# Ten one-hot products with the operands exchanged: three bfloat16 parts of the weights stationary, x moving 512 columns, sums transposed on TensorE

## The chip, the cores and the metric

One core of a Trainium2 chip runs the whole kernel. The metric is device time in microseconds (us); lower is better. Engines are named as in the profile: PE is TensorE's matmul, PEld its weight load, DVE is VectorE, ACT ScalarE, POOL GpSimd, SP SyncE, whose queue issues the large transfers.

## What is computed

Ten tables with 64 columns each, for a batch of 1024. The reference, cut to what matters:

```python
VOCABS = [12500, 6250, 2500, 1250, 625, 250, 1000, 500, 200, 100]
embs = [jnp.dot(x, w) for x, w in zip(xs, ws)]          # x: 1024 x v, w: v x 64, float32
emb_sum = embs[0]
q_emb = jnp.dot(xs[0] ** 2, ws[0] ** 2)
for i in range(1, len(xs)):
    emb_sum = emb_sum + embs[i]
    q_emb = q_emb + jnp.dot(xs[i] ** 2, ws[i] ** 2)
fm_ans = 0.5 * (emb_sum ** 2 - q_emb)
return jnp.concatenate([fm_ans] + embs, axis=-1)
```

Every x holds only zeros and ones.

## The kernel before, in words

The host hands x over transposed, so that the vocabulary lies on the partitions, 128 rows to a tile. There are 199 tiles, with the last tile of each table cut to a multiple of 16 rows. A tile of x is 128 x 1024 float32 (512 KB); one DMA brings a chunk of one or two tiles into one of SLOTS = 10 slots of `x_ring`. There are 108 chunks, and up to four of them make a group, whose weights come with one DMA from ACT's queue.

Because x is 0 or 1, the upper bfloat16 half of each float32 is x itself, and PE reads it in place (`upper_half`, a stride of two). A weight isn't exact in bfloat16, so each group's `pieces` are made of three summands. ACT squares the weights (`square`, L269), and POOL takes twice the rest that the upper half leaves (L326, L329). The tile `pieces` is laid out kind by kind, weights and squares apart: `[P, 3, 2, GROUP, D]`.

x is the stationary operand. For each tile and each of eight blocks of 128 batch rows PE loads x as 128 x 128 and moves the six parts of the tile through it, 384 columns (L363). The sums of a batch block lie in one PSUM bank, batch on the partitions. Tables are gathered in rounds (`ROUNDS`). The first round holds five small tables, and there and in the last round a tile is multiplied by 24 matmuls of 128 columns (L368), since the three kinds are added up in PSUM. At a round's end ACT copies bank after bank (`copy_out`, L290, L293), while PE's first matmul on each bank in the next round waits for its copy. DVE (`combine`) and POOL (`add_squares`) then add the parts up.

To prove that x holds nothing but 0 and 1, DVE counts ones in each chunk (L433) and ACT counts nonzeros (L276); a general path, which doesn't run with these inputs, stands behind a flag. A slot is filled again when PE, DVE and ACT have all read its chunk (the three waits in `load_x`).

The order on each engine is the order of the code; semaphores alone tie the engines together. The lines behind the two edits that matter most:

```python
            def load_w(group):
                if group.g >= BUFFERS:
                    act.wait_ge(x_multiplied, GROUPS[group.g - BUFFERS].end)
...
                    if c == 0 and group.g + LEAD + 1 < NGROUPS:
                        load_w(GROUPS[group.g + LEAD + 1])
                    if c == min(2, len(group.chunks) - 1) and group.g + LEAD < NGROUPS:
                        square(GROUPS[group.g + LEAD])
```

Of the kernel before, what the change touches and what calls it, by code (L numbers as in the profile page):

```python
# [17 lines left out]
PARTS = 6  # L18
PD = PARTS * D
# [9 lines left out]
ROUNDS = [  # L29
    [(8, [[1, 1]]), (6, [[2, 2, 2, 1, 1]]), (4, [[2, 2, 1]]), (9, [[1]]), (5, [[1, 1]])],  # L30
    [(3, [[2, 2, 2], [2, 1, 1]])],
    [(2, [FULL, [2, 2, 2], [2, 2, 1, 1]])],
    [(1, [FULL] * 6 + [[1]])],
    [(0, [FULL] * 12 + [[1, 1]])],
    [(7, [[2, 1, 1]])],
]
LAST_ROUND = len(ROUNDS) - 1
ORDER = [t for one in ROUNDS for t, _ in one]
LAST = ORDER[-1]
FIRSTS = len(ROUNDS[0])  # L40

Q_PLACE = FIRSTS + 1
PLACE = {t: n + 1 + (n >= FIRSTS) for n, t in enumerate(ORDER)}
CHUNK = max(FULL)
GROUP = sum(FULL)
SLOTS = 10

BUFFERS = 5
LEAD = 2
# [13 lines left out]
class Group:  # L63


    def __init__(self, g, round_, table, tile, sizes, k):
        self.g, self.round, self.table, self.tile = g, round_, table, tile
        self.tiles, self.buffer, self.turn = sum(sizes), g % BUFFERS, g // BUFFERS
        self.chunks, at = [], 0
        for n in sizes:  # L70
            self.chunks.append(Chunk(k + len(self.chunks), table, tile + at, n, at))
            at += n
        for chunk in self.chunks:
            chunk.group = self
        self.end = k + len(sizes)


def plan():
    groups, k = [], 0
    for n, one in enumerate(ROUNDS):  # L80
        for table, lists in one:
            tile = 0
            for sizes in lists:
                groups.append(Group(len(groups), n, table, tile, sizes, k))
                k, tile = groups[-1].end, tile + sum(sizes)
            assert tile == TILES[table] and lists[-1][-1] == 1
    return groups
# [5 lines left out]

BEGINS = [min(c.k for g in GROUPS if g.round == n for c in g.chunks) for n in range(len(ROUNDS))] + [NCHUNKS]
FLAG_MAX = P * NCHUNKS * CHUNK * BATCH


def rec_kernel(nc, xs, ws, out):
# [5 lines left out]
    with ExitStack() as ctx:  # L104
# [12 lines left out]
        pieces = [sb(f"pieces{i}", [P, 3, 2, GROUP, D], F32) for i in range(BUFFERS)]  # L117
        is_one = [sb(f"is_one{i}", [P, CHUNK * BATCH], U8) for i in range(2)]
        is_set = [sb(f"is_set{i}", [P, CHUNK * BATCH], U8) for i in range(2)]
# [6 lines left out]
        ones = sb("ones", [P, 1], F32)  # L126
        stages = [sb(f"stage{i}", [P, NB, PD], F32) for i in range(2)]
        low_sum = sb("low_sum", [P, NB, D], F32)
        q_low = sb("q_low", [P, NB, D], F32)
        q_round = sb("q_round", [P, NB, D], F32)  # L130
        emb_sum = sb("emb_sum", [P, NB, D], F32)
        results = sb("results", [P, NT + 2, NB, D], F32)
        q_total = results[:, Q_PLACE, :, :]
        g_weights = sb("g_weights", [P, 2, D], F32)

        w_landed = [sem(f"w_landed{i}") for i in range(BUFFERS)]
# [6 lines left out]
        pieces_ready = sem("pieces_ready")  # L143
        constants = sem("constants")
        bank_summed = sem("bank_summed")
        bank_copied = sem("bank_copied")
        combined = sem("combined")
        q_combined = sem("q_combined")
        added = sem("added")
        q_added = sem("q_added")  # L150
        half_read = sem("half_read")
        fm_ready = sem("fm_ready")
        last_emb = sem("last_emb")
# [17 lines left out]
        lower, upper = slice(0, NB // 2), slice(NB // 2, NB)  # L171

# [7 lines left out]
        def upper_half(chunk):  # L180

            return in_slot(chunk.slot, chunk.n * BATCH).bitcast(BF16).rearrange(
                "p (t b h) -> p t b h", h=2, b=BATCH)[0:chunk.rows, :, :, 1]

        def piece(group, kind):
            return pieces[group.buffer][:, kind, :, 0:group.tiles, :]

        def piece_upper(group, kind):

            return pieces[group.buffer][:, kind].bitcast(BF16).rearrange(  # L190
                "p m t (d h) -> p m t d h", h=2)[:, :, 0:group.tiles, :, 1]

        def tile_parts(chunk, t):


            return pieces[chunk.group.buffer][0:chunk.rows, :, :, chunk.at + t].bitcast(BF16).rearrange(
                "p k m (d h) -> p k m d h", h=2)[:, :, :, :, 1]

        def wait_bank(eng, n, b):

            if b < NB - 1:
                eng.wait_ge(bank_summed, (NB - 1) * n + b + 1)
            else:
                eng.wait_ge(x_multiplied, BEGINS[n + 1])
# [3 lines left out]
        def _(sp):  # L208
            def load_x(chunk):
# [11 lines left out]
            for chunk in CHUNKS:  # L221
                load_x(chunk)

            for n, one in enumerate(ROUNDS[:-1]):
                sp.wait_ge(added, n + 1)
                for t, _ in one:
                    sp.dma_start(out[t + 1], results[:, PLACE[t], :, :]).then_inc(stored, 16)
# [5 lines left out]
            with sp.If(odd != 0):  # L233
# [15 lines left out]
                sp.dma_start(out[0], results[:, 0, :, :]).then_inc(stored, 16)  # L249
                for t in range(NT):  # L250
# [5 lines left out]
        def _(act):  # L256
# [38 lines left out]

            for group in GROUPS[:LEAD + 1]:
                load_w(group)
# [258 lines left out]
```

## Time and profile before

| | |
|---|---|
| Median of 3 runs | 298.21 us (297.61 to 298.63) |
| Profiled execution, its own time | 298.65 us |
| Its span, first to last instruction | 296.9 us |
| PE busy | 274.8 us (93%) |
| DVE, ACT, POOL busy | 252.5, 230.2, 114.3 us |
| DMA | 113.31 MB, mean 382 GB/s |

Busy time of PE counts matmuls that overlap in the pipeline as busy once. The span leaves out what lies around the instructions, here 1.75 us.

### The profile page before, as it was taken

The numbers are of one execution on the slowest core, as the hardware profiler recorded it, in microseconds if no ns is written. First come the engines' busy times: TensorE is split into PE (matmuls) and PEld (weight loads), VectorE is DVE, ScalarE is ACT, GpSimd is POOL, SyncE is SP. The second block draws the span as 40 slices with busy tenths as digits, with TensorE's granted clock in tenths as the row PEclk, the third lists the DMA queues.
The fourth block names the chain that finished last, engine by engine and source line by source line (L and its number), as shares of the span: only waits on it lengthen the run. The fifth ranks groups of instructions, "written<-read, shape, count | busy, mean of one in ns | idle before, by whom it ended". The sixth has DMA issues, their size and how long they took to land.

```text
span 296.9 us, 5042 instructions
## 1 busy us (share of the span) xinstructions
PE 274.8 (93%) x1946; PEld 169.1 (57%) x1946; DVE 252.5 (85%) x240; ACT 230.2 (78%) x291; POOL 114.3 (39%) x78
## 2 busy tenths in 40 slices
PE   0899779999999999999999999999999999999960
PEld 0899735555555555555555555555555555555660
DVE  3669776899999999997887899998988888987883
ACT  2868499899699878776897878877787788876741
POOL 0911427276518551313618532540451353112060
PEclk9999979999999999999999999999999999999995
DMA  7999999999999999999999999999999999999921
GB/s 241 409 378 367 413 361 383 418 415 309 411 416 417 418 423 414 418 425 300 400 420 414 422 416 417 420 420 418 418 418 421 418 419 419 414 417 280 389 94 75
DMA packets 21435, 113.31 MB, mean 382 GB/s; under 512 B 2656, under 2 KB 3808, under 8 KB 9760
## 3 DMA queue, kind: packets, MB, share of 16 engines
q1 hardware_dynamic: 16800, 106.18, 90.2%
q10 hardware_dynamic: 4608, 6.79, 6.5%
q8 instruction: 16, 0.26, 0.4%
q14 instruction: 11, 0.09, 0.1%
HBM read 110.07 MB, written 2.88 MB: 380 GB/s over the span
## 4 chain that ended last, share of the span: by engine, by line
PE 82%; DMA 10%; DVE 2%; ACT 2%; issue 1%; POOL 0%; ACTq 0%
PE sums L363 81%; DMA x_ring<-in_x_dram 6%; DMA pieces<-in_w_dram 4%; ACT stage L293 1%; PE sums L368 1%; DVE results L450 1%; DVE odd_counts L467 0%; ACT L269 0%; ACT is_set L276 0%; DVE emb_sum L477 0%; DVE low_sum L447 0%; DVE results L483 0%; DVE results L487 0%; DVE results L479 0%; POOL pieces L329 0%
## 5 line engine op out<-in xcount | busy, mean ns | idle before, releaser
L433 DVE TENSOR_SCALAR_CACHE_REDUCE is_one<-x_ring 128x2048 uint8<-128x2048 f32 (+3 forms) x108 | 225.5, 2114 | 37.2 <-DMA x_ring<-in_x_dram 36.9
L363 PE MATMUL sums<-pieces,x_ring 128*128 128x384 bf16 x1416 | 242.1, 332 | 3.8 <-ACT results L290 3.8
L276 ACT ACTIVATE is_set<-x_ring 128x2048 uint8<-128x2048 uint32 (+3 forms) x108 | 192.1, 1787 | 43.9 <-DMA x_ring<-in_x_dram 43.0
L363 PEld LDWEIGHTS sums<-pieces,x_ring 128*128 128x128 bf16 x1416 | 136.5, 97 | 109.1 <-POOL pieces L329 3.9
L326 POOL TENSOR_TENSOR pieces<-pieces 128x1024 f32<-128x1024 f32 (+5 forms) x31 | 48.5, 1566 | 160.1 <-ACT pieces L269 160.1
L329 POOL TENSOR_TENSOR pieces<-pieces 128x1024 f32<-128x1024 f32 (+5 forms) x31 | 49.2, 1588 | 2.4
L368 PE MATMUL sums<-pieces,x_ring 128*128 128x128 bf16 (+2 forms) x528 | 32.7, 225 | 8.4 <-POOL pieces L329 8.4
L368 PEld LDWEIGHTS sums<-pieces,x_ring 128*128 128x128 bf16 (+2 forms) x528 | 32.5, 100 | 8.6 <-issue 8.4
L276 ACT ACTIVATION_READ_ACCUMULATOR is_set<-x_ring 128x1 f32 (+2 forms) x108 | 21.7, 201 | 0.0
L269 ACT ACTIVATE pieces<-pieces 128x512 f32<-128x512 f32 (+5 forms) x31 | 16.8, 545 | 4.7 <-DMA pieces<-in_w_dram 4.7
L293 ACT ACTIVATE stage<-sums 128x384 f32<-128x384 f32 x32 | 12.7, 521 | 2.3 <-PE sums L363 2.3
L335 POOL TENSOR_TENSOR q_low<-stage 128x512 f32<-128x512 f32 x4 | 5.7, 1412 | 10.9 <-ACT stage L293 10.9
L433 DVE DVE_READ_ACCUMULATOR is_one<-x_ring 128x1 f32 (+2 forms) x108 | 8.8, 81 | 0.0
L450 DVE TENSOR_TENSOR results<-low_sum,stage 128x512 f32<-128x512 f32 x4 | 6.9, 1720 | 0.1
L453 DVE TENSOR_TENSOR emb_sum<-emb_sum,results 128x512 f32<-128x512 f32 x4 | 6.9, 1719 | 0.1
L338 POOL TENSOR_TENSOR q_round<-q_low,stage 128x512 f32<-128x512 f32 x4 | 5.5, 1370 | 0.3
L341 POOL TENSOR_TENSOR results<-results,q_round 128x512 f32<-128x512 f32 x4 | 5.5, 1363 | 0.3
L269 ACT ACT_TABLE_LOAD x1 | 1.3, 1283 | 5.4 <-DMA pieces<-in_w_dram 5.4
L447 DVE TENSOR_TENSOR low_sum<-stage 128x512 f32<-128x512 f32 x4 | 4.0, 990 | 1.0 <-ACT stage L293 1.0
L441 DVE TENSOR_REDUCE emb_sum<-results 128x512 f32<-128x2560 f32 x1 | 4.8, 4784 | 0.0
L313 ACT ACTIVATE results<-sums 128x256 f32<-128x256 f32 x2 | 0.8, 384 | 4.6 <-DVE results L479 4.6
L392 PE MATMUL sums<-ones,odd_total 128*1 128x1 f32 x2 | 0.2, 164 | 4.0 <-ACT results L313 4.0
(16 smaller groups left out, 8.8 us busy)
## 6 DMA issues: line engine op xcount, KB each, us to landing
x_ring<-in_x_dram SPq DMA_DIRECT2D x91, 1024.0 KB, 20.0
x_ring<-in_x_dram SPq DMA_DIRECT2D x10, 512.0 KB, 16.4
pieces<-in_w_dram ACTq DMA_DIRECT2D x20, 256.0 KB, 7.3
out_dram<-results SPq DMA_DIRECT2D x10, 256.0 KB, 13.1
x_ring<-in_x_dram SPq DMA_DIRECT2D x4, 448.0 KB, 16.6
x_ring<-in_x_dram SPq DMA_DIRECT2D x2, 320.0 KB, 11.5
pieces<-in_w_dram ACTq DMA_DIRECT2D x3, 192.0 KB, 7.9
x_ring<-in_x_dram SPq DMA_DIRECT2D x1, 384.0 KB, 18.8
```

The costliest lines, as they stand in the source:

```text
L269: nc.scalar.activation(whole[:, 1], whole[:, 0], ACT.Square).then_inc(squared, 1)
L276: nc.scalar.activation(is_set[chunk.k % 2][0:chunk.rows, 0:chunk.n * BATCH], x_of(chunk).bitcast(U32), ACT.Sign, accum_out=set_counts[0:ch ...
L293: nc.scalar.activation(stages[n % 2][:, b, :], sums[:, b, 0:PD], ACT.Copy).then_inc(bank_copied, 1)
L326: nc.gpsimd.tensor_tensor(piece(group, 1), piece(group, 0), piece_upper(group, 0), ALU.subtract).then_inc(rest_ready, 1)
L329: nc.gpsimd.tensor_tensor(piece(group, 2), piece(group, 1), piece_upper(group, 1), ALU.subtract).then_inc(pieces_ready, 1)
L335: nc.gpsimd.tensor_tensor(q_low[:, :, :], stage[:, :, 3 * D:4 * D], stage[:, :, 5 * D:], ALU.add).then_inc(q_combined, 1)
L338: nc.gpsimd.tensor_tensor(q_round[:, :, :], q_low[:, :, :], stage[:, :, D:2 * D], ALU.add).then_inc(q_combined, 1)
L363: return nc.tensor.matmul(sums[:, b, 0:PD], x, parts, start=first, stop=False, skip_group_check=True)
L368: last = nc.tensor.matmul(columns[:, at:q_at + 1:q_at - at, :], x, parts[:, kind], start=first and kind == 2, stop=False, skip_group_check ...
L433: nc.vector.tensor_scalar(is_one[chunk.k % 2][0:chunk.rows, 0:chunk.n * BATCH], x_of(chunk), 1.0, None, ALU.is_equal, ALU.add, accum_out=o ...
L450: nc.vector.tensor_tensor(emb, low_sum[:, :, :], stage[:, :, 0:D], ALU.add).then_inc(combined, 1)
L453: nc.vector.tensor_tensor(emb_sum[:, :, :], emb_sum[:, :, :], emb, ALU.add).then_inc(added, 1)
```

## The change

The operands change places. A tile's weights and squares are now side by side (`[P, 3, GROUP, 2 * D]`), 128 columns to a kind, and each kind is the stationary operand of two matmuls, through which 512 columns of x move. All three kinds are added up in PSUM, in a pair of banks, with the embedding's 64 columns and the squares' 64 on the partitions and the batch along the bank. Each table has its own pair, in turn one of two. After each table ACT copies the pair to SBUF (`copy_sums`), PE transposes it in eight blocks of 128 x 128 float32 (`turn`) into one of two other pairs, ACT copies the embedding out of it (`copy_emb`) and DVE adds embedding and squares to a running total (`add`). These steps are put off by COPY_AFTER, TURN_AFTER and ADD_AFTER chunks from the table's end.

The three weight parts need a buffer that has both halves, so the weights land in `loaded` (3 buffers) and ACT makes two passes, a copy and a square, into `pieces` (4 buffers). SLOTS goes from 10 to 12, the rounds go, and the order of the tables is another.

```diff
-ROUNDS = [
-    [(8, [[1, 1]]), (6, [[2, 2, 2, 1, 1]]), (4, [[2, 2, 1]]), (9, [[1]]), (5, [[1, 1]])],
-    [(3, [[2, 2, 2], [2, 1, 1]])],
...
-    [(7, [[2, 1, 1]])],
-]
-SLOTS = 10
-BUFFERS = 5
-LEAD = 2
+ORDER = [
+    (8, [[1, 1]]),
+    (9, [[1]]),
+    (5, [[1, 1]]),
+    (4, [[2, 2, 1]]),
+    (7, [[2, 1, 1]]),
+    (3, [[2, 2, 2], [2, 1, 1]]),
...
+    (0, [FULL] * 12 + [[1, 1]]),
+    (6, [[2, 2, 2, 1, 1]]),
+]
+SLOTS = 12
+WHOLES = 3
+PAIRS = 4
+AHEAD = 3
+COPY_AFTER, TURN_AFTER, ADD_AFTER = 2, 3, 5
+def due(k, after):
+    return [n for n in range(NT - 1) if min(END[n] - 1 + after, NCHUNKS - 1) == k]
...
+            def square(group):
+                act.wait_ge(w_landed[group.whole], 16 * (group.turn + 1))
+                if group.g >= PAIRS:
+                    act.wait_ge(x_multiplied, GROUPS[group.g - PAIRS].end)
+                w = loaded[group.whole][:, 0:group.tiles, :]
+                nc.scalar.activation(piece(group, 0)[:, :, 0:D], w, ACT.Copy).then_inc(squared, 1)
+                nc.scalar.activation(piece(group, 0)[:, :, D:], w, ACT.Square).then_inc(squared, 1)
+            def copy_sums(n):
+                act.wait_ge(x_multiplied, END[n])
+                if n >= 2:
+                    act.wait_ge(sums_turned, n - 1)
+                at = summing(n, 0)
+                nc.scalar.activation(turned[n % 2][:, :].rearrange("p (a b) -> p a b", a=2),
+                                     sums[:, at:at + 2, :], ACT.Copy).then_inc(sums_copied, 1)
...
+                    if c == min(1, len(group.chunks) - 1):
+                        if group.g + AHEAD < NGROUPS:
+                            load_w(GROUPS[group.g + AHEAD])
+                    if c == min(2, len(group.chunks) - 1) and group.g + AHEAD - 1 < NGROUPS:
+                        square(GROUPS[group.g + AHEAD - 1])
+                    for n in due(chunk.k, COPY_AFTER):
+                        copy_sums(n)
+                    for n in due(chunk.k, ADD_AFTER):
+                        copy_emb(n, ORDER[n][0])
...
+            def multiply(chunk):
+                group, n = chunk.group, chunk.group.place
+                pe.wait_ge(x_landed[chunk.slot], 16 * (chunk.turn + 1))
+                if chunk.k == BEGIN[n] and n >= 2:
+                    pe.wait_ge(sums_copied, n - 1)
+                x = x_upper(chunk)
+                for t in range(chunk.n):
+                    for kind in (2, 1, 0):
+                        w = piece_upper(group, kind)[0:chunk.rows, chunk.at + t, :]
+                        first = chunk.k == BEGIN[n] and t == 0 and kind == 2
+                        for half in range(2):
+                            at = t * BATCH + half * HALF
+                            last = nc.tensor.matmul(sums[:, summing(n, half), :], w,
+                                                    x[:, at:at + HALF], start=first, stop=False,
+                                                    skip_group_check=True)
+                last.then_inc(x_multiplied, 1)
+            def turn(n, blocks):
+                for b in range(blocks.start, blocks.stop):
+                    last = nc.tensor.transpose(turning(n)[:, b, :, :],
+                                               turned[n % 2][:, b * P:(b + 1) * P], identity[:, :])
+                last.then_inc(sums_turned, 1)
```

What this does to the order is seen at two places. The first is PE's start. Before, it multiplied three chunks with nothing but x and `pieces` to wait for:

```order
L368 MATMUL sums<-pieces,x_ring 128x2x64 [waits x_landed0,pieces_ready,constants]
L368 MATMUL sums<-pieces,x_ring 128x2x64 x23
L368 MATMUL sums<-pieces,x_ring 128x2x64 [waits x_landed1]
L368 MATMUL sums<-pieces,x_ring 128x2x64 x23
L368 MATMUL sums<-pieces,x_ring 128x2x64 [waits x_landed2,pieces_ready]
L368 MATMUL sums<-pieces,x_ring 128x2x64 x47
```

Of the changed kernel, PE from its first matmul (`turned` is the SBUF copy of the sums, `identity` a unit matrix):

```order
L361 MATMUL sums<-x_ring,pieces 128x512 [waits parts_ready,x_landed0,unit_ready,constants]
L361 MATMUL sums<-x_ring,pieces 128x512 x5
L361 MATMUL sums<-x_ring,pieces 128x512 [waits x_landed1]
L361 MATMUL sums<-x_ring,pieces 128x512 x5
L361 MATMUL sums<-x_ring,pieces 128x512 [waits x_landed2,parts_ready]
L361 MATMUL sums<-x_ring,pieces 128x512 x5
L361 MATMUL sums<-x_ring,pieces 128x512 [waits sums_copied,x_landed3,parts_ready]
L361 MATMUL sums<-x_ring,pieces 128x512 x5
L361 MATMUL sums<-x_ring,pieces 128x512 [waits x_landed4]
L361 MATMUL sums<-x_ring,pieces 128x512 x5
L368 MATMUL sums<-identity,turned 128x128 [waits sums_copied]
L368 MATMUL sums<-identity,turned 128x128 x7
```

A tile is now 6 matmuls of 512 columns, and the fourth chunk (the third table's first) waits for `sums_copied`, the copy of the first table's sums.

The second place is ACT's queue at the same time. Before, between the counts of the second and the fourth chunk:

```order
L276 ACTIVATE is_set,set_counts<-x_ring 80x1024 [waits x_landed1]
L269 ACTIVATE pieces<-pieces 128x320 [waits w_landed2]
L276 ACTIVATE is_set,set_counts<-x_ring 128x2048 [waits set_counted,x_landed2]
L262 DMA pieces<-in_w_dram 128x128
L276 ACTIVATE is_set,set_counts<-x_ring 128x2048 [waits set_counted,x_landed3]
```

And in the changed kernel, from the second chunk's count to the first `copy_sums` (L287):

```order
L276 ACTIVATE is_set,set_counts<-x_ring 80x1024 [waits x_landed1]
L258 DMA loaded<-in_w_dram 128x320 [waits squared]
L268 ACTIVATE pieces<-loaded 128x2x64 [waits w_landed2]
L269 ACTIVATE pieces<-loaded 128x2x64
L276 ACTIVATE is_set,set_counts<-x_ring 112x1024 [waits set_counted,x_landed2]
L258 DMA loaded<-in_w_dram 128x256 [waits squared]
L268 ACTIVATE pieces<-loaded 128x5x64 [waits w_landed0]
L269 ACTIVATE pieces<-loaded 128x5x64
L276 ACTIVATE is_set,set_counts<-x_ring 128x1024 [waits set_counted,x_landed3]
L287 ACTIVATE turned<-sums 128x1024 [waits x_multiplied]
```

The weights that the copy of 128x5x64 waits for are issued one chunk earlier on the same queue (the row with 128x320), and the copy of the first table's sums stands behind that wait.

## Rows read from the trace of the kernel before

**Rows 1.** The page: span and PE's busy time
```profile
span 296.9 us, 5042 instructions
PE 274.8 (93%) x1946; PEld 169.1 (57%) x1946; DVE 252.5 (85%) x240; ACT 230.2 (78%) x291; POOL 114.3 (39%) x78
PE 82%; DMA 10%; DVE 2%; ACT 2%; issue 1%; POOL 0%; ACTq 0%
```

**Rows 2.** Windows, core 0: start:end, length, busy (instructions) by engine, clock, DMA, GB/s
```profile
8.40:13.00 4.60, 4.55 (x44) 4.58 (x45) 2.90 (x3) 3.76 (x8) 4.52 (x3) 1.00 1.03 416
39.20:43.40 4.20, 4.13 (x16) 1.79 (x17) 3.22 (x3) 4.20 (x8) 0.00 (x0) 0.64 1.07 352
43.40:280.00 236.60, 236.60 (x1395) 134.15 (x1394) 212.64 (x189) 195.01 (x232) 94.69 (x57) 1.00 1.02 404
```

**Rows 3.** Timeline of PE and PEld: start, us, engine, what
```profile
150.25 129.83 PEld L363 LDWEIGHTS sums<-pieces,x_ring 128*128 128x128 bf16 x765 [0.27 <-ACT stage L293]
281.17 5.67 PE L368 MATMUL sums<-pieces,x_ring 128*128 128x128 bf16 x96
281.29 5.55 PE L368 MATMUL sums<-pieces,x_ring 128*128 128x128 bf16 x94
```

**Rows 4.** Waits: us in total, times, longest
```profile
PE sums L368 <- POOL pieces L329: 8.4, 1, 8.4
PE sums L363 <- ACT results L290: 3.8, 1, 3.8
SPq L216 <- PE sums L363: 163.0, 80, 4.9
```

**Rows 5.** Timeline of DVE's counts, late in the run, with idle time before
```profile
252.19 2.29 DVE L433 TENSOR_SCALAR_CACHE_REDUCE is_one<-x_ring 128x2048 uint8<-128x2048 f32 x1 [0.20 <-DMA x_ring<-in_x_dram]
254.68 2.29 DVE L433 TENSOR_SCALAR_CACHE_REDUCE is_one<-x_ring 128x2048 uint8<-128x2048 f32 x1 [0.20 <-DMA x_ring<-in_x_dram]
277.90 2.29 DVE L433 TENSOR_SCALAR_CACHE_REDUCE is_one<-x_ring 128x2048 uint8<-128x2048 f32 x1 [0.98 <-DMA x_ring<-in_x_dram]
```

**Rows 6.** DMA: share in 40 slices, then issues with KB each, us to landing
```profile
DMA  7999999999999999999999999999999999999921
x_ring<-in_x_dram SPq DMA_DIRECT2D x91, 1024.0 KB, 20.0
pieces<-in_w_dram ACTq DMA_DIRECT2D x2, 32.0 KB, 7.0
```

**Rows 7.** Timeline of ACT: the count of the first chunk
```profile
7.40 1.04 ACT L276 ACTIVATE is_set<-x_ring 128x1024 uint8<-128x1024 uint32 x1
```

**Rows 8.** Groups by form: count, busy, mean ns, idle before
```profile
L269 ACT ACTIVATE pieces<-pieces 128x512 f32<-128x512 f32 (+5 forms) x31 | 16.8, 545 | 4.7 <-DMA pieces<-in_w_dram 4.7
...
L293 ACT ACTIVATE stage<-sums 128x384 f32<-128x384 f32 x32 | 12.7, 521 | 2.3 <-PE sums L363 2.3
L313 ACT ACTIVATE results<-sums 128x256 f32<-128x256 f32 x2 | 0.8, 384 | 4.6 <-DVE results L479 4.6
L269 ACT ACTIVATE pieces<-pieces 128x320 f32<-128x320 f32 x1 | 0.5, 471 | 0.8 <-DMA pieces<-in_w_dram 0.8
L269 ACT ACTIVATE pieces<-pieces 128x128 f32<-128x128 f32 x3 | 0.9, 299 | 0.0
L363 PEld LDWEIGHTS sums<-pieces,x_ring 128*128 128x128 bf16 x1384 | 133.4, 97 | 106.8 <-POOL pieces L329 3.9 <-ACT stage L293 1.5 <-ACT results L290 1.3
L477 DVE TENSOR_TENSOR emb_sum<-sums,emb_sum 128x256 f32<-128x256 f32 x2 | 0.8, 415 | 0.0
L483 DVE SCALAR_TENSOR_TENSOR results<-emb_sum 128x512 f32<-128x512 f32 x1 | 0.7, 691 | 0.0
```

**Rows 9.** The chain that ended last, its last steps: start, us, what
```profile
288.99 0.41 DVE emb_sum L477
291.16 0.69 DVE results L487
```

More of the change, by code:

```diff
@@ L63, with __init__ @@
 class Group:
-    def __init__(self, g, round_, table, tile, sizes, k):
-        self.g, self.round, self.table, self.tile = g, round_, table, tile
-        self.tiles, self.buffer, self.turn = sum(sizes), g % BUFFERS, g // BUFFERS
+    def __init__(self, g, place, table, tile, sizes, k):
+        self.g, self.place, self.table, self.tile = g, place, table, tile
+        self.tiles, self.whole, self.turn, self.pair = sum(sizes), g % WHOLES, g // WHOLES, g % PAIRS
         self.chunks, at = [], 0
@@ L79, in plan @@
     groups, k = [], 0
[L80 to L86, printed above, removed]
+    for n, (table, lists) in enumerate(ORDER):
+        tile = 0
+        for sizes in lists:
+            groups.append(Group(len(groups), n, table, tile, sizes, k))
+            k, tile = groups[-1].end, tile + sum(sizes)
+        assert tile == TILES[table] and lists[-1][-1] == 1
     return groups
@@ L92 @@
 NGROUPS, NCHUNKS = len(GROUPS), len(CHUNKS)
-BEGINS = [min(c.k for g in GROUPS if g.round == n for c in g.chunks) for n in range(len(ROUNDS))] + [NCHUNKS]
+BEGIN = [min(g.chunks[0].k for g in GROUPS if g.place == n) for n in range(NT)]
+END = [max(g.end for g in GROUPS if g.place == n) for n in range(NT)]
 FLAG_MAX = P * NCHUNKS * CHUNK * BATCH
+def due(k, after):
+    return [n for n in range(NT - 1) if min(END[n] - 1 + after, NCHUNKS - 1) == k]
 def rec_kernel(nc, xs, ws, out):
@@ L219, in load_x @@
                              ).then_inc(x_landed[chunk.slot], 16)
[L221 to L227, printed above, removed]
+            for n, (t, _) in enumerate(ORDER[:-1]):
+                sp.wait_ge(emb_copied, n + 1)
+                sp.dma_start(out[t + 1], results[:, t + 1, :, :]).then_inc(stored, 16)
             sp.wait_ge(fm_ready, 1)
@@ L248, in _ @@
                 sp.wait_ge(g_done, 1)
[L249 to L251 removed]
+                for n in range(NT + 1):
+                    sp.dma_start(out[n], results[:, n, :, :]).then_inc(stored, 16)
                 sp.wait_ge(stored, 2 * 16 * (NT + 1))
@@ L345, in _ @@
[L345 to L350 removed]
+                                        ALU.subtract).then_inc(parts_ready, 1)
         @block.tensor
         def _(pe):
[L355 to L356 removed]
@@ L358, in products @@
-            def products(chunk, b, t, first):
-                x = upper_half(chunk)[:, t, b * P:(b + 1) * P]
-                parts = tile_parts(chunk, t)
-                if chunk.table not in places:
-                    return nc.tensor.matmul(sums[:, b, 0:PD], x, parts, start=first, stop=False,
-                                            skip_group_check=True)
-                at, q_at = places[chunk.table]
-                columns = sums[:, b, :].rearrange("p (r d) -> p r d", d=D)
-                for kind in (2, 1, 0):
-                    last = nc.tensor.matmul(columns[:, at:q_at + 1:q_at - at, :], x, parts[:, kind],
-                                            start=first and kind == 2, stop=False,
-                                            skip_group_check=True)
-                return last
+            def multiply(chunk):
[8 more added lines that the diff above has]
+                        first = chunk.k == BEGIN[n] and t == 0 and kind == 2
+                        for half in range(2):
+                            at = t * BATCH + half * HALF
[3 more added lines that the diff above has]
+                last.then_inc(x_multiplied, 1)
```

269 lines of the change are left out of this document (105 added, 164 removed).

## The prediction

> **What bounds the kernel now.** I read the page first: PE is busy for 274.8 of 296.9 us and carries 82% of the chain that ended last [rows 1]. PE's busy time can hide waits, so I went to its timeline. From 150.25 us on, 765 weight loads follow each other in 129.83 us with no wait between them: 129.83 / 765 = 0.170 us for a matmul of 384 columns [rows 3]. At the end 94 matmuls of 128 columns take 5.55 us, of which the last one's own record is some 0.2, so 0.0574 us each [rows 3]. PE waits twice: 8.4 us before its first matmul and 3.8 us for the copy at the first round's end [rows 4]. The rest is issue rate. The windows give the clock's price. From 8.40 to 13.00 only 44 short matmuls run, where 4.6 / 0.0574 = 80 would fit, so the engine, idle before, works at the lower of its two levels, 1.2 GHz, and loses 2.1 us (the clock column doesn't tell it there; the spacing of 0.10 us does). After the 3.8 us wait the window 39.20 to 43.40 grants 0.64 and holds 17 loads for 24.7 that would fit, 1.3 us lost [rows 2].
>
> These parts make up PE's whole chain: 8.4 + 2.1 + 528 x 0.0574 + 3.8 + 1.3 + 1416 x 0.170 = 286.6 us, and PE does end at 281.17 + 5.67 = 286.8 [rows 3]. So PE's issue is the bound. What is close behind? The 16 DMA engines are all but fully busy until 280 us, and a 1 MB load takes 20.0 us to land because some eight stand in line [rows 6]. DVE starts its counts as they land, 2.49 us apart when no weights come in between [rows 5], against 16 x 0.170 = 2.72 us of PE for the same chunk. SP waits for PE 80 times, 163 us in all [rows 4], and still the DMA engines have work. From the count at 277.90, which waited for its landing, two half-size chunks were still to land: the last lands at about 277.9 + 2 x 1.25 = 280.4 us. So the second bound lies only 6 us below the first, and that caps any gain on PE.
>
> **The matmuls.** Columns don't change: 8 x 384 = 6 x 512 = 3072 a tile. Only what a matmul costs above its columns can change. At 2.4 GHz (the window's clock is 1.00 [rows 2]) 384 columns are 160.0 ns and 128 are 53.3 ns; the rows have 169.7 and 57.4, so 9.7 and 4.1 ns over [rows 3]. These two points allow two readings. In the first, every run of 64 elements costs something: the 384 columns are gathered in six runs, the 128 in two, so 1.4 ns a run and 1.3 ns a matmul; 512 columns of x are one run: 213.3 + 2.7 = 216 ns. In the second, the surplus grows with the columns: (169.7 - 57.4) / 256 = 0.4387 ns a column, 226 ns for 512. These are my two ends. I take 216 ns, since in the second reading a matmul without columns would still cost 1.2 ns and there would be no reason why the rate, at the lower level, is exactly the columns' own. 199 tiles x 6 = 1194 matmuls: 257.9 us (270 by the other end). Before it was 30.3 + 240.7 = 271.0, so 13.1 us go.
>
> A rule bears on this. The Trainium skill, "TensorE: Matmul & The Clock Gate", section "Back-to-back issue gap", gives N / 2.4 + 2.5 ns: 55.8 and 162.5 ns here, so both rows lie above it, by 1.6 and 7.2 ns. For 512 columns in one run it would give 215.8 ns, and the sum would be 257.7 us.
>
> **The transposes.** They are new: 9 tables x 8 = 72 in PE's stream, 8 more at the end. No row has a float32 matmul of this size. Below: one pass of 128 columns, 57 ns [rows 3]. Above: four such passes, 230 ns. The stationary operand is float32 data, 128 columns, and a bfloat16 load of that shape is 97 ns long [rows 8]; I take 110 ns, a load that a 53 ns matmul can't cover. 72 x 0.11 = 7.9 us (4.1 to 16.6).
>
> **The start.** ACT copies and squares the first group's weights instead of squaring them in place: 0.3 us more (299 ns for 128 columns [rows 8]), so PE begins at 8.7 us. The lower clock again costs 2.1. Three chunks of one tile are 18 matmuls, 3.9 us, and PE is done with them at 14.7. It then meets the new wait of the order shown above. ACT ends the count of the second chunk at about 7.6 + 2 x 1.1 = 9.8 us [rows 7], issues the weights of the fourth table, counts the third chunk, and then stops until these weights land: 7.0 us after issue for a small load in this stage [rows 6], 16.8. Copy and square of 320 columns, 2 x 0.47 [rows 8], count of the fourth chunk 1.1, then the copy of 1024 columns out of PSUM: 384 and 256 columns took 521 and 384 ns [rows 8], so 1.07 ns a column, 1.2 us. That is 20.2, and PE's fourth chunk starts at 20.3: a stall of 5.6 us, after which the clock is down again (1.3 us, as after the 3.8 us wait). The old stall of 3.8 + 1.3 at the first round's end goes, since nothing but the next-but-one table waits for a copy now. Queued behind ACT's wait are the counts; they hold back slots that PE still holds too.
>
> **Work beside it.** ACT's second pass over the weights (31 activations, 16.8 us for the first pass [rows 8]) and 10 copies of 1.2 us stand against 40 bank copies that go, which took some 16; DVE's adds are one of 1024 columns for each table in place of three or more of 512; POOL loses `add_squares`. ACT's 230.2 us [rows 1] become about 249 with the ten embedding copies, 85% of the span, and a count of 1.9 us hides behind PE's 2.6 us a chunk. If that cover were gone, each table's copy would add 1.2 us. The three-chunk delay hides the copies at the later tables; I set 0.5 us for what leaks through at ten boundaries.
>
> **The sum.** 8.7 + 2.1 + 5.6 + 1.3 + 0.5 + 257.9 + 7.9 = 284.0 us for PE's last product. The transfers allow 280.4 + 6 x 0.216 = 281.7, so PE still decides, just. The tail: ACT's copy of half the sums 0.65, four transposes with the pipeline's 0.2 together 0.65, DVE's add of 512 columns 0.7 (415 ns for 256 [rows 8]), the other half 0.7, two final operations of 0.69 [rows 8, 9] and 0.2 of gaps: 4.3 us. The old tail ended at 291.85 [rows 9], and the span 5.05 later; that stays. 284.0 + 4.3 + 5.05 = 293.3, against 296.9. The profiled execution took 298.65, 1.75 over its span and 0.44 above the runs' median. 298.21 - 3.6 = 294.6 us, 1.2% faster.
>
> **Rival 1: the transposes are dear (slower).** A float32 operand in four passes is 230 ns: 72 x 0.12 + 0.5 = 9.1 us more, 303.7 us. One mechanism, on PE's stream between tables; it turns the sign where 76 transposes eat the 3.6 us, at 157 ns each. For it speaks that PE is the bound, against it that nothing has to be multiplied. In numbers of a page: the Trainium skill, same page, section "PE-mode transpose", reports about 275 ns for one in a kernel, bfloat16. That would be 306 us. The same page's list of terms calls the transpose mode 4 times faster for float32, which fits my value better. No run here has shown either yet. 18%.
>
> **Rival 2: the surplus is by column (slower).** 226 ns: 12 us more on PE, 306.6 us; with transposes at 57 ns 302.8. The sign turns at 219 ns. 16%.
>
> **Rival 3: the transfers decide (faster by the most).** With transposes at 57 ns PE would be done at 280.2, under the 281.7 that the last landing allows. 281.7 + 9.35 = 291.0 span, 292.3 us. Nothing in this change moves a byte less, so no result should lie below that by more than a few tenths. 17%.
>
> **Rival 4: nothing to be seen.** ACT's queue now holds copies that wait for PE (`copy_sums`), and behind them copies and squares of later weights and the counts that free slots. Late by a microsecond at three or four of the small tables, they eat the gain: 297.3 to 299.1 us. For it: the small tables follow each other within 2 to 4 chunks, less than the put-off of 5. Against it: each sits behind PE's own backlog. 10%.
>
> My forecast as it stands, 293 to 297, has 39%. **Numbers.** Within 0.3% (about what this kernel's runs can tell from no change, 0.9 us) is rival 4, 10%. Faster: forecast and rival 3 with a part of their spread, 56%. Slower: rivals 1 and 2, 34%. The range goes from rival 3's 292.0 to rival 1's 304.0, which leaves out the dearest cases.
>
> **What the profile would show.** Long runs of matmuls of 512 columns spaced 216 ns (rival 2: 226). Eight transposes after each table's third following chunk, 0.9 us for eight (rival 1: 1.8). One wait of PE for ACT's copy of the sums at 14 to 20 us, 5 to 6 us long, and a granted clock under 1.00 behind it. DVE's counts starting well ahead of PE, DMA busy to 280. Last product at 284. The forecast is wrong if PE waits for ACT at the later tables, if the clock falls around the transposes, or if moving x out of the ring that DMA, ACT and DVE use at the same time makes a matmul slower than its columns.

## The result and the profile after

The changed kernel takes 300.95 us (median of 4 runs, 300.79 to 301.17), the kernel before in the same comparison 297.91 us (4 runs, 296.78 to 298.63). The ratio is 1.0106, with a 95% interval of 1.0072 to 1.0140: 1% slower. The forecast was 294.6 us and 1.2% faster. The time lies inside the stated range, and the sign is wrong.

The page of the changed kernel answers to [rows 1] and [rows 6]: span, busy times, the DMA engines' share in 40 slices, the engines' shares of the chain that ended last.

```profile
span 299.4 us, 3740 instructions
PE 282.6 (94%) x1276; PEld 125.6 (42%) x1276; DVE 239.2 (80%) x234; ACT 238.6 (80%) x302; POOL 96.9 (32%) x67
DMA  7999999999999999999999999999999999999501
PE 92%; DMA 2%; ACT 1%; DVE 1%; issue 0%; ACTq 0%; DVEq 0%
```

PE's share of the chain rose from 82 to 92%, and nothing else of note is left on it. The next view is that chain of the changed kernel (start, us, what): its start, its longest stretches and its end.

```profile
7.09 6.96 DMA loaded<-in_w_dram
14.08 0.48 ACT pieces L268
...
17.00 3.37 PE sums L361 x12
20.37 0.87 PE sums L368 x8
...
153.59 0.87 PE sums L368 x8
154.47 132.50 PE sums L361 x588
286.97 0.87 PE sums L368 x8
287.85 2.72 PE sums L361 x12
290.56 0.02 issue
290.59 0.61 ACT turned L317
...
291.33 0.64 PE sums L368 x4
...
292.06 1.30 DVE total L467 x2
...
293.39 0.70 DVE results L470
...
294.11 0.69 DVE results L473
```

The reader finds the answer in one row: 588 matmuls of 512 columns follow each other in 132.50 us, so 225.3 ns each, where the forecast counted on 216. Eight transposes take 0.87 us, 109 ns each, as forecast. The tail from 290.57 to 294.80 is the forecast's too.

DVE's timeline near the end shows how far PE lags behind the transfers, in answer to [rows 5]. The last two chunks have landed before 280 us, yet PE finishes with the last of them at 290.57:

```profile
276.38 2.29 DVE L434 TENSOR_SCALAR_CACHE_REDUCE is_one<-x_ring 128x2048 uint8<-128x2048 f32 x1 [1.08 <-DMA x_ring<-in_x_dram]
...
278.59 1.21 DVE L434 TENSOR_SCALAR_CACHE_REDUCE is_one<-x_ring 128x1024 uint8<-128x1024 f32 x1
...
279.73 1.22 DVE L434 TENSOR_SCALAR_CACHE_REDUCE is_one<-x_ring 112x1024 uint8<-112x1024 f32 x1
```

The start went another way than foreseen. PE's timeline (start, us, what, idle time before):

```profile
8.70 7.84 PE L361 MATMUL sums<-x_ring,pieces 128*128 128x512 bf16 x18 [8.70 <-POOL pieces L342]
17.00 3.37 PE L361 MATMUL sums<-x_ring,pieces 128*128 128x512 bf16 x12 [0.46 <-ACT turned L287]
20.21 1.03 PE L368 MATMUL sums<-identity,turned 128*128 128x128 f32 x8
```

18 matmuls take 7.84 us here. The last one's own record is some 0.6 us long, and the starts are 427 ns apart, which is 512 columns at 1.2 GHz to the nanosecond (512 / 1.2 = 426.7). The clock column of a window over them reads 1.00 all the same, so here too it is the spacing that tells the level. The lower level lasts until about 18.1 us, worked out from how many of the next 12 matmuls must be slow for 3.37 us. The foreseen wait for ACT's copy is there, but only 0.46 us of it.

### The profile page after: what moved, and what is told of

The parts are those of the page before. It is cut to its first block, busy times and chain, and to the rows that moved or that the text cites. A ratio compares the mean times of both kernels' runs of the same rounds, so it can differ in the third digit from the quotient of the medians.

```text
span 299.4 us, 3740 instructions
## 1 busy us (share of the span) xinstructions
PE 282.6 (94%) x1276; PEld 125.6 (42%) x1276; DVE 239.2 (80%) x234; ACT 238.6 (80%) x302; POOL 96.9 (32%) x67
## 4 chain that ended last, share of the span: by engine, by line
PE 92%; DMA 2%; ACT 1%; DVE 1%; issue 0%; ACTq 0%; DVEq 0%
PE sums L361 89%; PE sums L368 3%; DMA loaded<-in_w_dram 2%; DVE total L467 0%; ACT is_set L276 0%; ACT turned L287 0%; DVE results L470 0%; DVE results L473 0%; ACT turned L317 0%; ACT pieces L268 0%; ACTq L258 0%; ACT pieces L269 0%; DVEq L466 0%
## 5 line engine op out<-in xcount | busy, mean ns | idle before, releaser
L361 PE MATMUL sums<-x_ring,pieces 128*128 128x512 bf16 (+1 forms) x1194 | 275.0, 391 | 9.2 <-POOL pieces L342 8.7
L361 PEld LDWEIGHTS sums<-x_ring,pieces 128*128 128x128 bf16 (+1 forms) x1194 | 116.6, 98 | 163.4 <-issue 15.3
L339 POOL TENSOR_TENSOR pieces<-pieces 128x1024 f32<-128x1024 f32 (+5 forms) x31 | 48.2, 1556 | 167.0 <-ACT pieces L269 167.0
L342 POOL TENSOR_TENSOR pieces<-pieces 128x1024 f32<-128x1024 f32 (+5 forms) x31 | 48.2, 1556 | 2.4
L446 DVE TENSOR_TENSOR total<-sums,total 128x1024 f32<-128x1024 f32 x8 | 9.8, 1224 | 17.9 <-ACT results L292 17.9
L268 ACT ACTIVATE pieces<-loaded 128x512 f32<-128x512 f32 (+5 forms) x31 | 16.6, 535 | 3.2 <-DMA loaded<-in_w_dram 3.2
L287 ACT ACTIVATE turned<-sums 128x1024 f32<-128x1024 f32 x9 | 9.2, 1017 | 10.1 <-PE sums L361 10.1
L269 ACT ACTIVATE pieces<-loaded 128x512 f32<-128x512 f32 (+5 forms) x31 | 16.5, 533 | 0.0
L292 ACT ACTIVATE results<-sums 128x512 f32<-128x512 f32 x9 | 5.4, 598 | 8.4 <-PE sums L368 8.4
L368 PE MATMUL sums<-identity,turned 128*128 128x128 f32 x80 | 10.4, 272 | 0.8 <-ACT turned L317 0.8
L368 PEld LDWEIGHTS sums<-identity,turned 128*128 128x128 f32 x80 | 9.2, 140 | 3.2 <-issue 1.3
L467 DVE TENSOR_TENSOR total<-sums,total 128x512 f32<-128x512 f32 x2 | 1.3, 686 | 1.8 <-PE sums L368 1.8
## 6 DMA issues: line engine op xcount, KB each, us to landing
out_dram<-results SPq DMA_DIRECT2D x10, 256.0 KB, 12.9
```

Of the source, the lines that this page charges most:

```text
L268: nc.scalar.activation(piece(group, 0)[:, :, 0:D], w, ACT.Copy).then_inc(squared, 1)
L269: nc.scalar.activation(piece(group, 0)[:, :, D:], w, ACT.Square).then_inc(squared, 1)
L287: nc.scalar.activation(turned[n % 2][:, :].rearrange("p (a b) -> p a b", a=2), sums[:, at:at + 2, :], ACT.Copy).then_inc(sums_copied, 1)
L292: nc.scalar.activation(results[:, t + 1, :, :], turning(n)[:, :, 0, :], ACT.Copy).then_inc(emb_copied, 1)
L339: nc.gpsimd.tensor_tensor(piece(group, 1), piece(group, 0), piece_upper(group, 0), ALU.subtract).then_inc(rest_ready, 1)
L342: nc.gpsimd.tensor_tensor(piece(group, 2), piece(group, 1), piece_upper(group, 1), ALU.subtract).then_inc(parts_ready, 1)
```

## Two theories, and what tells them apart

My theory after this result: each matmul is too long because of how PE reads its moving operand. It takes the upper halves of float32 data, so every second bfloat16 (a stride of two), and pays for that in proportion to the columns. The rivals: the number of separate runs of elements matters (the first reading of *The matmuls*); the stationary operand, now also read with a stride, is slow to load; or PE is disturbed because it moves x out of the memory that DMA, ACT and DVE use at the same time. A theory of the start stands apart from these: that the lower clock there is what can be won back.

One row of each kernel measures the disputed time, so the rows come first. A window of 100 us in which only the largest table runs holds no transposes and no copies of banks. Dividing it by the number of weight loads (PEld, one for each matmul) gives the time of a matmul. The columns are those of [rows 2].

The kernel before, 100 us / 588 = 170 ns for 384 columns with a stride of two, in six runs:

```profile
165.00:265.00 100.00, 100.00 (x590) 57.04 (x588) 91.35 (x79) 80.52 (x85) 35.56 (x20) 1.00 1.02 418
```

The changed kernel, 100 / 444 = 225 ns for 512 columns with a stride of two, in one run:

```profile
165.00:265.00 100.00, 100.00 (x446) 43.02 (x444) 87.27 (x79) 83.95 (x97) 33.11 (x19) 1.00 1.02 413
```

## Experiment 1: the moving operand adjacent

Of the changed kernel:

```diff
-            return in_slot(chunk.slot, chunk.n * BATCH).bitcast(BF16).rearrange(
-                "p (e h) -> p e h", h=2)[0:chunk.rows, :, 1]
+            return in_slot(chunk.slot, chunk.n * BATCH).bitcast(BF16)[0:chunk.rows, 0:chunk.n * BATCH]
```

> The changed kernel, but PE's moving operand is 512 adjacent bfloat16 elements of the slot in place of every second one; the products are therefore of other data, and the output is not the reference's. Theory S (the 12 ns above the columns come from reading x with a stride of two): matmuls 215 to 217 ns apart, PE's work 11 us shorter, so that the transfers decide; about 292.5 us. Theory C (they come from sharing the ring's memory with DMA, ACT and DVE) and theory W (from the weight load): still 225 ns and 301 us.

Measured: 293.06 us (4 runs, 292.53 to 293.81) against 298.70; ratio 0.9799 (0.9758 to 0.9841). The same window has 464 loads, 100 / 464 = 215.5 ns:

```profile
165.00:265.00 100.00, 99.53 (x456) 45.24 (x464) 85.03 (x75) 83.14 (x95) 33.75 (x20) 1.00 1.02 413
```

This one edit takes some 8 to 9 us off the changed kernel (0.9799 against 1.0106). Its chain is still 82% PE, but near its end PE waits for data, as its timeline shows, so the transfers have become a bound at PE's own height:

```profile
275.58 2.77 PE L360 MATMUL sums<-x_ring,pieces 128*128 128x512 bf16 x12 [0.62 <-DMA x_ring<-in_x_dram]
```

## Experiment 2: the stationary operand adjacent

```diff
-                        w = piece_upper(group, kind)[0:chunk.rows, chunk.at + t, :]
+                        w = ones[:, :].bitcast(BF16)[0:chunk.rows, 0:2 * D]
```

> The changed kernel, but the stationary operand is always the same 128 adjacent bfloat16 elements of a constant tile, so that the products are of other data. Theory W (the weight load with its stride costs the 12 ns): 216 ns a matmul and about 292.5 us. Theories S and C: 225 ns and 301 us as before the edit.

Measured: 301.45 us (10 runs, 300.19 to 302.40), ratio 1.0086 (1.0056 to 1.0117), in which the changed kernel's 1.0106 lies. The window, with 100 / 445 = 225 ns:

```profile
165.00:265.00 100.00, 99.43 (x437) 42.57 (x445) 87.64 (x77) 84.30 (x97) 33.40 (x19) 1.00 1.02 413
```

How the stationary operand is read costs nothing here.

## Experiment 3: each transpose twice

```diff
-                for b in range(blocks.start, blocks.stop):
+                for b in [*range(blocks.start, blocks.stop)] * 2:
```

> The changed kernel with each table's eight transposes made twice. If PE's issue is the bound from end to end, the 80 added transposes of 0.109 us come on top: 8.7 us, about 309.7 us. If slack at the table ends hides them: under 303 us.

Measured: 311.15 us (4 runs, 309.12 to 311.86), ratio 1.0380 (1.0320 to 1.0439). PE's timeline has sixteen in 1.91 us; less the last one's own 0.27, that is 0.109 us each:

```profile
160.93 1.91 PE L368 MATMUL sums<-identity,turned 128*128 128x128 f32 x16
```

80 more of them are 8.7 us, and the ratio rose by 0.027 over the changed kernel's, 8.2 us of 298. The profiled spans differ by 10.1 us (309.5 against 299.4). Of this 1.4 us lies ahead of the first transpose (21.59 against 20.21 us), where the lower clock lasted longer, and 8.7 us are left for the transposes. So their price is shown on the whole kernel too: 8 to 9 us, which outweighs by far the 2.0 us by which the matmuls became cheaper.

## Experiment 4: the stride kept, the shared memory left

PE moves x from a tile that nothing else touches after it was filled:

```diff
+        x_still = sb("x_still", [P, CHUNK * BATCH], F32)
...
-            return in_slot(chunk.slot, chunk.n * BATCH).bitcast(BF16).rearrange(
+            return x_still[:, 0:chunk.n * BATCH].bitcast(BF16).rearrange(
```

> The changed kernel, but PE's moving operand comes, with the same stride of two, from a tile of ones that nobody writes after the start or reads beside PE; the products are of other data, and all waits stay. Theory C: 216 ns a matmul and about 292.5 us. Theories S and W: 225 ns and 301 us.

Measured: 301.02 us (10 runs, 300.64 to 302.71), ratio 1.0081 (1.0056 to 1.0105), and 100 / 444 = 225 ns:

```profile
165.00:265.00 100.00, 99.42 (x436) 43.00 (x444) 87.40 (x79) 84.04 (x97) 33.12 (x19) 1.00 1.02 413
```

That PE reads the same tile as DMA, ACT and DVE at the same time costs nothing. The new tile still lies in the memory that they all use, but so does the ring in experiment 1, where adjacent reads took 215.5 ns. So that rival falls.

## Experiments 5 and 6: runs and stride apart, in the kernel before

Both change the 384 columns that the kernel before moves, and take them from a tile of ones. Experiment 5 keeps six runs of 64 but makes their elements adjacent. Experiment 6 makes one run of them but keeps the stride:

```diff
-            return pieces[chunk.group.buffer][0:chunk.rows, :, :, chunk.at + t].bitcast(BF16).rearrange(
-                "p k m (d h) -> p k m d h", h=2)[:, :, :, :, 1]
+            return still[0:chunk.rows].bitcast(BF16)[:, :, :, 0:D]
```

```diff
-            return pieces[chunk.group.buffer][0:chunk.rows, :, :, chunk.at + t].bitcast(BF16).rearrange(
+            return still[0:chunk.rows].bitcast(BF16).rearrange(
                 "p k m (d h) -> p k m d h", h=2)[:, :, :, :, 1]
```

> The kernel before, but its moving operand comes from a constant tile of ones: six runs of 64 adjacent bfloat16 elements (two runs in the 128-column matmuls), in place of the weights' parts with a stride of two; the products are of other data. Theory S (stride): 162 to 164 ns a matmul of 384 columns in place of 170, PE's work 9 to 10 us shorter, and since the last landing allows no more than 5 us, about 293 us. The forecast's reading (runs): still 170 ns and 298 us.

> The kernel before, but its moving operand comes from a constant tile of ones as one run of 384 elements with a stride of two; the products are of other data. Theory S (stride): still 170 ns and 298 us. The forecast's reading (runs): 163 ns and about 293 us.

The window of experiment 5 has 100 / 616 = 162.3 ns, that of experiment 6 again 100 / 588 = 170 ns. First 5, then 6:

```profile
165.00:265.00 100.00, 100.00 (x617) 60.23 (x616) 90.40 (x78) 79.84 (x84) 35.82 (x20) 1.00 1.02 419
```

```profile
165.00:265.00 100.00, 100.00 (x590) 57.04 (x588) 91.37 (x79) 80.53 (x85) 35.83 (x20) 1.00 1.02 418
```

So the runs cost nothing, and the stride costs all that lies above 162.3 ns; the 2.3 ns between that and the columns' own 160.0 stay with either way of reading. The times surprised me: 297.91 us for experiment 5, ratio 1.0006 (0.9981 to 1.0031), and 298.62 us for 6, ratio 1.0029 (1.0000 to 1.0058). With experiment 5 each large matmul is 7.7 ns shorter, 10.9 us over 1416 of them, and the kernel is no faster. Its table of waits shows two places where this goes, one of 5.1 us where the kernel before waits 3.8 [rows 4], and one of 2.7 us at 147.84 that the kernel before doesn't have. Behind the second the granted clock is 0.59 until 152 us, which costs some 1.8 us more (752 matmuls in 124.04 us). Its timelines of PE, ACT and DVE near the end show a third:

```profile
PE sums L363 <- ACT results L290: 5.1, 1, 5.1
PE sums L363 <- ACT stage L293: 3.1, 2, 2.7
```

```profile
272.56 5.38 PE L363 MATMUL sums<-still,x_ring 128*128 128x384 bf16 x32 [0.68 <-DMA x_ring<-in_x_dram]
280.97 7.15 PE L368 MATMUL sums<-still,x_ring 128*128 128x128 bf16 x96 [3.04 <-ACT stage L293]
```

```profile
278.45 1.91 ACT L276 ACTIVATE is_set<-x_ring 128x2048 uint8<-128x2048 uint32 x1 [1.04 <-DMA x_ring<-in_x_dram]
...
280.36 3.14 ACT L293 ACTIVATE stage<-sums 128x384 f32<-128x384 f32 x8
```

```profile
283.53 0.69 DVE L448 TENSOR_TENSOR low_sum<-stage 128x512 f32<-128x512 f32 x1 [0.50 <-ACT stage L293]
...
291.22 0.69 DVE L488 SCALAR_TENSOR_TENSOR results<-results 128x512 f32<-128x512 f32 x1
```

PE is through with the last large table at 277.94. But ACT must first wait for the landing at 278.45 and count that chunk, and only then does it copy the banks. DVE can't start on them before 283.53 and ends at 291.91, where the kernel before ended at 291.85 [rows 9]. In the structure of before, the last landing together with the hand-over of the eight banks is a second bound at the same height as PE's. I had seen the landing as the second bound, but had put it 6 us below the first by counting only PE's work behind it. The chain of before says so too: it leaves PE at 280.15 us for ACT's copies and then DVE, and PE's last 96 matmuls, which my sum had counted up to 286.8 us, are not on it.

## Experiment 7: ACT writes x as bfloat16, PE moves that

ACT makes a sign of each x for its count anyway. Here it writes this as bfloat16 into one of four tiles, and PE moves adjacent columns from there. The slots of the ring no longer wait for PE, but ACT stands between landing and PE:

```diff
-        is_set = [sb(f"is_set{i}", [P, CHUNK * BATCH], U8) for i in range(2)]
+        is_set = [sb(f"is_set{i}", [P, CHUNK * BATCH], BF16) for i in range(SETS)]
...
-                    sp.wait_ge(x_multiplied, chunk.k - SLOTS + 1)
...
+                if chunk.k >= SETS:
+                    act.wait_ge(x_multiplied, chunk.k - SETS + 1)
...
-                pe.wait_ge(x_landed[chunk.slot], 16 * (chunk.turn + 1))
+                pe.wait_ge(set_counted, chunk.k + 1)
```

> The changed kernel, with ACT writing the sign of x, which is x itself here, as bfloat16 into one of four tiles, and PE moving these 512 adjacent columns in place of every second element of the slot. All of the reference is computed. Theory S: 216 ns a matmul; PE trails ACT, so the end of the last product is one count of ACT (1.1 us) behind the last landing: 293 to 294.5 us. If the tie of ACT to PE through four tiles costs (ACT waits for PE, and with it the counts that free slots): above 296 us.

Measured: 294.99 us (4 runs, 294.15 to 295.22), ratio 0.9895 (0.9847 to 0.9943). PE's timeline near the end, two of its waits and the last stretch:

```profile
254.57 10.74 PE L362 MATMUL sums<-is_set,pieces 128*128 128x512 bf16 x48 [0.62 <-ACT is_set L277]
...
278.02 2.76 PE L362 MATMUL sums<-is_set,pieces 128*128 128x512 bf16 x12 [0.59 <-ACT is_set L277]
...
281.50 2.75 PE L362 MATMUL sums<-is_set,pieces 128*128 128x512 bf16 x12
```

That is 0.5 us above the range expected. In the end PE follows ACT, whose pass over a chunk of two tiles takes 1.9 us, and is done at 284.25, some 6 us earlier than in the changed kernel, but 2.4 later than in experiment 1 (281.8).

## Experiment 8: 40 matmuls ahead of the first

PE multiplies ones while it waits for the first weights, so that the clock is up before the work begins:

```diff
             pe.wait_ge(unit_ready, 1)
+            for i in range(WARM):
+                nc.tensor.matmul(sums[:, 7, 0:256], ones[:, :].bitcast(BF16)[:, 0:P],
+                                 ones[:, :].bitcast(BF16), start=True, stop=True,
+                                 skip_group_check=True)
```

> The changed kernel with 40 matmuls of 256 columns on a tile of ones before the first product, while PE would wait for weights. If the lower clock over the first 22 products is paid in full (22 x 0.2 us), PE ends 4.4 us sooner and the time is 296.5 us; if the early waits for ACT take it back, 299 to 301 us.

Measured: 302.66 us (4 runs, 302.10 to 303.70), ratio 1.0163 (1.0111 to 1.0216): slower than the changed kernel (1.0106) if anything, and above both times that I had named. PE's timeline and a window of its start:

```profile
1.59 6.16 PE L376 MATMUL sums<-ones 128*128 128x256 bf16 x40 [1.59 <-POOL identity L335]
8.25 4.24 PE L362 MATMUL sums<-x_ring,pieces 128*128 128x512 bf16 x18 [0.50 <-POOL pieces L343]
16.70 5.28 PE L362 MATMUL sums<-x_ring,pieces 128*128 128x512 bf16 x12 [4.21 <-ACT turned L288]
```

```profile
15.00:22.00 7.00, 5.30 (x14) 2.04 (x15) 2.88 (x4) 7.00 (x11) 4.27 (x4) 0.51 1.01 408
```

The 18 matmuls now take 4.24 us, not 7.84, so the first half of the idea works. But they are done at 12.49, and the copy of the first sums isn't: the stall which *The start* had foreseen appears, 4.2 us long, and the granted clock behind it is 0.51. So the 3.6 us won are lost on the spot, and the lower level is paid a second time. In the changed kernel the slow clock had hidden this wait.

## Experiment 9: the sign tiles, but the last twelve chunks from the ring

Experiment 7, except that for the last 12 chunks PE moves x from the ring with the stride, as soon as it lands, and ACT no longer waits for PE there:

```diff
+            if chunk.k >= NCHUNKS - SLOTS:
+                return in_slot(chunk.slot, chunk.n * BATCH).bitcast(BF16).rearrange(
+                    "p (e h) -> p e h", h=2)[0:chunk.rows, :, 1]
+            return is_set[chunk.k % SETS][0:chunk.rows, 0:chunk.n * BATCH]
...
+                if chunk.k >= NCHUNKS - SLOTS:
+                    pe.wait_ge(x_landed[chunk.slot], 16 * (chunk.turn + 1))
+                else:
+                    pe.wait_ge(set_counted, chunk.k + 1)
```

> The kernel of e7, but for the last 12 chunks PE reads x out of its slot again, with the stride of two, as soon as it has landed, and ACT no longer waits for PE there. In e7 PE ended 5.8 us behind the last landing and in e1 3.8. If ACT's count between landing and product is the difference, the time is 293 to 293.8 us; if the price of the stride in 11 table tiles' worth of matmuls (some 20 chunks' tiles x 6 x 9.5 ns, 1.1 us) or the other waits of the end decide, 294.5 us or more.

Measured: 292.54 us (6 runs, 291.83 to 293.54) against 298.58; ratio 0.9790 (0.9753 to 0.9827). It computes all of the reference and beats both kernels, by 2.1% and about 3%. That is half a microsecond below the range expected. The page's shares of its chain, and PE's timeline before its end:

```profile
DMA 59%; PE 24%; issue 5%; DVE 3%; ACT 1%; POOL 1%; ACTq 0%; DVEq 0%
```

```profile
276.43 2.88 PE L368 MATMUL sums<-x_ring,pieces 128*128 128x512 bf16 x12 [0.16 <-DMA x_ring<-in_x_dram]
279.15 1.03 PE L375 MATMUL sums<-identity,turned 128*128 128x128 f32 x8
280.02 2.87 PE L368 MATMUL sums<-x_ring,pieces 128*128 128x512 bf16 x12
```

PE now follows the landings and finishes at 282.9. The chain is 59% DMA: this is the state that rival 3 spoke of, whose floor was 292.3 us.

## Experiment 10: experiment 8 with the weights asked for earlier

A fourth buffer for landing weights, and four groups asked for at the start:

```diff
-WHOLES = 3
+WHOLES = 4
...
-            for group in GROUPS[:AHEAD]:
+            for group in GROUPS[:LOADS]:
                 load_w(group)
```

> The kernel of e8 (40 matmuls on ones ahead of the first product), with a fourth buffer for landing weights and the first four groups' weights asked for at the start. In e8 PE met ACT's wait for the fourth table's weights (4.2 us) and fell to the lower clock again for 6.8 us. If that wait took the gain, it shrinks to about 1 us, the clock stays, and PE ends 6 to 7 us sooner than in e8: 295.5 to 297 us. If the clock falls again whatever the wait, 299 us or more.

Measured: 297.46 us (10 runs, 297.06 to 297.94), ratio 0.9969 (0.9945 to 0.9992). Against experiment 8's 1.0163 that is 5 to 6 us, against the changed kernel 3.5 to 4. PE's timeline:

```profile
8.27 4.24 PE L363 MATMUL sums<-x_ring,pieces 128*128 128x512 bf16 x18 [0.70 <-POOL pieces L344]
13.45 2.87 PE L363 MATMUL sums<-x_ring,pieces 128*128 128x512 bf16 x12 [0.94 <-ACT turned L289]
```

The wait has shrunk from 4.21 to 0.94 us, and 12 matmuls behind it take 2.87 us, so the clock stayed up. The matmuls ahead won nothing by themselves (experiment 8), and together with the earlier weights they win back about 4 us of the start. The earlier weights alone were not run; the wait that they could shorten in the changed kernel is 0.46 us long.

## Why the prediction was wrong, step by step

PE's time to its last product, as *The sum* had it and as the trace has it:

| Term | Forecast, us | Trace, us | Trace's number from |
|---|---|---|---|
| Start of PE | 8.7 | 8.7 | timeline |
| Lower clock | 2.1 + 1.3 | 4.4 | 18 x 0.225 is 4.1 of 7.84; 12 x 0.225 is 2.7 of 3.37 |
| Stall for ACT's copy | 5.6 | 0.5 | timeline |
| Leak at tables | 0.5 | 0.0 | no such wait in the chain |
| 1194 matmuls | 257.9 | 269.0 | 1194 x 0.2253 |
| 72 transposes | 7.9 | 7.9 | 9 x 0.87 |
| Last product | 284.0 | 290.5 | chain: 290.57 |
| Tail | 4.3 | 4.2 | 290.57 to 294.80 |
| Rest of the span | 5.05 | 4.6 | 299.4 - 294.80 |
| Span | 293.3 | 299.4 | page |

**The step that failed** is the choice in *The matmuls*. Both readings were on the table, and I took the first, "every run of 64 elements costs something", for 216 ns. The second, by column, gave 226 and was the right one: 225.3. That is 11.1 us. The miss of the span is only 6.1 us, because the stall came out 5.1 us smaller. That the time fell inside the range is therefore luck: with the measured spacing and the stall as I had it, the sum gives 305.7 us, above the range's end at 304.0, and rival 2's own 306.6 lay outside it as well.

My argument against the second reading was that the rate at the lower level is exactly the columns' own. That is true (427 ns for 512), but it says nothing about the higher level: the stride costs only there. Experiments 1, 5 and 6 settle it. Adjacent, the gap is 162.3 ns for 384 columns and 215.5 for 512; with the stride it is 170.0 and 225.3. So 7.7 and 9.8 ns, between 4 and 5% of the matmul. The stationary side (experiment 2), the shared memory (4) and the runs (5, 6) are ruled out. What in the chip makes the stride dear wasn't tried.

The Trainium skill, "TensorE: Matmul & The Clock Gate", section "Back-to-back issue gap", gives N / 2.4 + 2.5 ns, 162.5 and 215.8 ns for these sizes. The adjacent reads agree with it to 0.3 ns. For reads with a stride the rule is too low here, by 7.5 and 9.5 ns. The row of before had already shown the first of these, and carrying the rule over to 512 columns meant taking that surplus as a matter of the old shape alone.

**The transposes** were right at 109 ns, and rival 1 was wrong. In the groups by line a transpose's mean is 272 ns, which is how long the record of one is. They overlap, and only the spacing (0.87 us for eight) is what PE pays. The Trainium skill's number for one, about 275 ns (same page, "PE-mode transpose"), is for bfloat16, lies near the 272 of these float32 records, and would have overstated the sum by 12 us.

**The start** was mis-sized, in the moment at which ACT's copy of the first sums ends: 16.85 us, not 20.2. The load of the fourth table's weights took the 7.0 us of [rows 6], but it was issued at 7.09, not at 9.8. In the order it stands behind two counts of ACT. Yet ACT's timeline shows it issued before either of them ran, at the moment when its own semaphore, a square of the first group, was given:

```profile
6.77 0.29 ACT L269 ACTIVATE pieces<-loaded 128x128 f32<-128x128 f32 x1
...
7.09 0.33 ACTq L258 DMA_DIRECT2D loaded<-in_w_dram  x1
...
7.26 1.04 ACT L276 ACTIVATE is_set<-x_ring 128x1024 uint8<-128x1024 uint32 x1
...
8.30 1.04 ACT L276 ACTIVATE is_set<-x_ring 80x1024 uint8<-80x1024 uint32 x1
...
15.85 1.00 ACT L287 ACTIVATE turned<-sums 128x1024 f32<-128x1024 f32 x1
```

So in this trace ACT's queue came to the DMA before the two counts ahead of it had run. PE goes on at about 17 us whatever its clock was: in experiment 4, where 18 matmuls took only 6.07 us, it waited 2.31 us for the copy and went on at 17.33. So the lower clock and the stall aren't two terms of a sum, as I had them, but cover each other up to the end of the copy. Experiment 8 shows the stall bare, 4.2 us.

**Work beside it** and **the tail** held: ACT was busy for 238.6 us where I had 249, and the DMA engines until 280. **Rival 2** was the right mechanism, with 306.6 us as its price. That was too dear by 5.7 us, since it kept the forecast's 5.6 us stall. **Rival 3** is not what happened here, but experiments 1 and 9 reach it, at 293.1 and 292.5 us. **What bounds the kernel** was half right: PE's issue was a bound before, and experiment 5 shows the second bound at the same height, not 6 us below it.

Set against the kernel before, the change reads so: matmuls 271.0 to 269.0 (-2.0), transposes +7.9, start 15.6 to 13.6 (-2.0), the end behind PE's last product 10.1 to 8.8 (-1.2). Together +2.7 against the spans' +2.5. With adjacent reads the matmuls would have been 257 (1194 x 0.2155). The last item compares two ends of PE and not two chains, since before the change the chain had left PE at 280.15.

What stays open is why the lower clock at the start lasts as long as it does. It lasted until 13.0 us before and until 18.1 us after the change. Among kernels whose start is nearly the same, it was 12.3, 12.9 and 12.6 us in experiments 2, 4 and 9, but 20.9, 20.7 and 21.3 us in 3, 7 and 1. Up to the end of ACT's copy this costs nothing. Behind it, it does: the next 12 matmuls took 2.87 us in experiment 4, 3.37 in the changed kernel and 4.60 in experiment 3.

## What to carry to other kernels

Fit the gap between matmuls against every property that could carry the surplus, and if two fits pass through the same two rows, measure one matmul of the new shape before counting on either: 10 ns on 1194 matmuls is the whole result here. When PE is the bound, give it a moving operand whose elements are adjacent, best as a by-product of a pass that another engine makes anyway. A gain on the bounding engine pays only as far as the next bound, which includes the hand-over behind the last landing (experiment 5) and waits that a slow start had hidden (experiment 8).

## What the runs showed of the hardware

- At 2.4 GHz PE pays for a moving bfloat16 operand with a stride of two: 225 against 215.5 ns for 512 columns, 170 against 162.3 ns for 384. At 1.2 GHz the stride costs nothing: 512 such columns take 427 ns, and the first 18 matmuls take 7.84 us with it and, in experiment 1, without it.
- The same stride in the stationary operand (225 ns with and without), six runs in place of one (170 ns both, with the stride), and other engines at work on the same tile (225 ns both) cost nothing that shows.
- Float32 transposes of 128 x 128 follow each other every 109 ns, while the record of one is 272 ns long. The clock stayed up through 16 of them (granted 1.00 during and behind them in experiment 3).
- A wait of PE can bring the clock down again: the granted clock was 0.51 behind one of 4.21 us (experiment 8) and 0.59 behind one of 2.68 us (experiment 5), but 1.00 behind one of 2.63 us (experiment 2).
